# Eight instead of twelve shared units ahead of the experts, and the gather of their results in four parts

## What is computed

```
def _L1_cond_ref(x, router_logits, skill_gate, skill_up, skill_down, shared_gate, shared_up, shared_down):
    def _gemma_mlp(x, gate_w, up_w, down_w):
        g = jnp.einsum('bsh,hi->bsi', x, gate_w)
        u = jnp.einsum('bsh,hi->bsi', x, up_w)
        return jnp.einsum('bsi,ih->bsh', jax.nn.gelu(g, approximate=True) * u, down_w)
    rw = jax.nn.softmax(router_logits, axis=-1)
    w, sel = jax.lax.top_k(rw, 2)
    w = w / w.sum(axis=-1, keepdims=True)
    ...
    # out = sum over the two chosen experts of w * _gemma_mlp(x, ...)
    out = out + _gemma_mlp(x, shared_gate, shared_up, shared_down)
    return out
...
x = x + _L0_ffn_ref(_L0_cond_ref(x, ...), ...)
x = x + _L1_ffn_ref(_L1_cond_ref(x, ...), ...)     # act_qdq needs the largest |value| of its whole input
```

## Time and profile before

| | us |
|---|---|
| median of 3 runs | 492.7 (492.66 to 494.01) |
| the profiled execution, own time | 496.16 |
| its span, first to last instruction | 494.4 |
| PE busy | 388.2 (79%) |
| DVE busy | 337.5 (68%) |
| ACT busy | 268.0 (54%) |
| POOL busy | 253.1 (51%) |
| share of PE in the chain of work that ended last | 63% |
| mean granted clock of PE | 0.893 |

### The profile page before, as it was taken

The page is one execution under the profiler, slowest core; times in us unless marked ns, Lnnn a source line. Parts: engine busy times, 40 slices in busy tenths (PEclk is TensorE's granted clock), DMA queues, the critical chain, the costliest instruction groups (busy, mean ns, idle before and its releaser), DMA issues.

```text
span 494.4 us, 8506 instructions
## 1 busy us (share of the span) xinstructions
PE 388.2 (79%) x2550; PEld 340.5 (69%) x2550; DVE 337.5 (68%) x562; ACT 268.0 (54%) x402; POOL 253.1 (51%) x444
## 2 busy tenths in 40 slices
PE   2888948999999999999999999899487870000197
PEld 1655736779999999999999998676255640000197
DVE  2686546757789776776777766457555788979643
ACT  2565765655545445455454456454364688749360
POOL 2576841466677575665756201666134018976140
PEclk9997976999999999999999999899688995555599
DMA  8989770005776777767777515300000000000012
GB/s 268 356 267 315 247 297 1 1 0 204 264 254 230 278 237 256 262 233 272 245 241 273 205 34 196 156 1 1 0 0 0 1 0 0 0 1 0 0 65 106
DMA packets 31212, 71.26 MB, mean 144 GB/s; under 512 B 3904, under 2 KB 20032, under 8 KB 25920
## 3 DMA queue, kind: packets, MB, share of 16 engines
q1 hardware_dynamic: 28976, 66.33, 38.8%
q0 software_dynamic: 288, 4.19, 2.1%
q10 hardware_dynamic: 1904, 0.20, 0.3%
HBM read 55.12 MB, written 15.60 MB: 143 GB/s over the span
## 4 chain that ended last, share of the span: by engine, by line
PE 63%; DVE 18%; ACT 9%; POOL 4%; DMA 2%; issue 2%; ACTq 1%; POOLq 0%; DVEq 0%
PE ps L178 46%; PE ps L710 10%; DVE S L196 7%; DVE G L187 4%; PE ps L713 4%; PE ps L175 3%; DMA G<-yscr,sidx 2%; ACT G L184 1%; ACT ps L184 1%; POOL XCl L187 1%; ACT xnT L184 1%; ACT C_i L184 1%; POOL Hl L187 1%; ACT U L184 1%; DVE G L193 1%
## 5 line engine op out<-in xcount | busy, mean ns | idle before, releaser
L665 POOL CAST xg<-XT 128x64 fp32r x312 | 114.2, 413 | 60.2 <-PE ps L178 53.9
L184 ACT ACTIVATE Gb<-ps 128x512 f32<-128x512 f32 x110 | 65.8, 598 | 105.9 <-PE ps L178 105.2
L178 PE MATMUL ps<-xg,Wr 128*128 128x256 f32 x936 | 120.0, 284 | 0.0
L187 DVE TENSOR_TENSOR HbS<-Gb,ps 128x512 f32<-128x512 f32 x110 | 75.4, 686 | 62.4 <-PE ps L178 62.1
L178 PEld LDWEIGHTS ps<-xg,Wr 128*128 128x128 f32 x936 | 114.3, 190 | 0.1
L184 ACT ACTIVATE Hh<-HbS 128x512 fp32r<-128x512 f32 x110 | 68.9, 627 | 13.9 <-DVE HbS L187 13.9
L710 PE MATMUL ps<-WD,Hh 128*128 x312 | 74.3, 328 | 0.0
L713 PE MATMUL ps<-WD,Hl 128*128 x312 | 69.4, 223 | 0.0
L187 DVE TENSOR_TENSOR Hl<-HbS,Hh 128x512 fp32r<-128x512 f32 x90 | 65.1, 734 | 2.2
L713 PEld LDWEIGHTS ps<-WD,Hl 128*128 128x128 f32 x312 | 59.8, 192 | 0.0
L710 PEld LDWEIGHTS ps<-WD,Hh 128*128 128x128 f32 x312 | 59.0, 189 | 0.0
(11 more groups left out here) (181 smaller groups left out, 688.7 us busy)
## 6 DMA issues: line engine op xcount, KB each, us to landing
Wr<-wscr SPq DMA_DIRECT2D x39, 1024.0 KB, 5.1
wscr<-wst SPq DMA_DIRECT2D x16, 512.0 KB, 4.3
yscr<-Yb SPq DMA_DIRECT2D x39, 128.0 KB, 3.0
stg<-n_L_cond_skill_gate_dram SPq DMA_DIRECT2D x8, 256.0 KB, 5.7
stg<-in_L_cond_skill_up_dram SPq DMA_DIRECT2D x8, 256.0 KB, 3.8
stg<-n_L_cond_skill_down_dram SPq DMA_DIRECT2D x8, 256.0 KB, 4.4
out_dram<-X SPq DMA_DIRECT2D x7, 256.0 KB, 2.0
X<-in_x_dram SPq DMA_DIRECT2D x3, 512.0 KB, 6.5
```

What stands on the lines that cost most here:

```text
L178: return lambda e: e.matmul(o_, l, r, start=start, stop=stop, skip_group_check=True)
L184: return lambda e: e.activation(o_, i_, func, **kw)
L187: return lambda e: e.tensor_tensor(o_, a, b, op)
L665: k_xg[i] = pool.do(lambda e, s=s: e.tensor_copy(xg[:, i % XR, :, T * s:T * s + T], XT[:, :, :, bass.ds(regb[i][s], 1)].rearrange("p a t o ...
```

## The change

J0 goes from 3 to 2, so HK from 12 to 8: units 8 to 11 run behind the experts instead of ahead of them. EARLY goes from 6 to 4. The gather is cut into four parts of eight tokens (two groups j each), in the order of parts 2, 3, 0, 1; that makes eight indirect DMAs of 512 KB instead of two of 2 MB, each pair with its own semaphore, and needs eight index columns in `sidx` instead of two. Groups are weighed in every second step from 14 to 28, in the order 4, 5, 6, 7, 0, 1, 2, 3, and turned one step later. The weights' turns stay three steps behind HK.

```diff
-J0 = 3
-EARLY = J0 + 3
+J0 = 2
+EARLY = J0 + 2
...
                 if i == 4:
-                    tok["sidx"] = dve.do(cp(sidx[:, 0:2], S[:, 42:44]), d_)
+                    for p in range(4):
+                        tok["sidx"] = dve.do(ts(sidx[:, 2 * p:2 * p + 2], S[:, 42:44], 4.0, float(p), MUL, ADD), d_)
...
-        s_g = sem("s_g")
+        l_g = {}
         pool.wait(*y_tok, d_sidx, *moe_done)
-        l_g = None
-        for k, D in enumerate((G0, G1)):
-            l_g = pool.dma(lambda e, k=k, D=D: e.indirect_dma_start(
-                out=D[:, :, :].rearrange("p t c -> p (t c)"), out_offset=None, in_=yscr[:, :],
-                in_offset=bass.IndirectOffsetOnAxis(ap=sidx[:, k:k + 1], axis=0)), s_g, k + 1)
+        for p in (2, 3, 0, 1):
+            s_g = sem(f"s_g{p}")
+            for k, D in enumerate((G0, G1)):
+                l_g[p] = pool.dma(lambda e, k=k, D=D, p=p: e.indirect_dma_start(
+                    out=D[:, 8 * p:8 * p + 8, :].rearrange("p t c -> p (t c)"), out_offset=None,
+                    in_=yscr.rearrange("n (q c) -> (n q) c", q=4),
+                    in_offset=bass.IndirectOffsetOnAxis(ap=sidx[:, 2 * p + k:2 * p + k + 1], axis=0)), s_g, k + 1)
...
-            k_g[j] = pool.do(ts(flat(G0, j), flat(G0, j), S[:, 38:39], 0.0, MUL, ADD), l_g, d_w01)
+            k_g[j] = pool.do(ts(flat(G0, j), flat(G0, j), S[:, 38:39], 0.0, MUL, ADD), l_g[j // 2], d_w01)
...
-        weighs = {20: 0, 21: 1, 23: 2, 24: 6, 26: 3, 27: 7, 29: 4, 30: 5}
+        weighs = {14: 4, 16: 5, 18: 6, 20: 7, 22: 0, 24: 1, 26: 2, 28: 3}
+        turns = {n + 1: j for n, j in weighs.items()}
...
-            if n in (15, 16, 17):
-                turn_wf(n - 15)
+            if n in (11, 12, 13):
+                turn_wf(n - 11)
```

More of the change, by code:

```diff
@@ L802, in program @@
         a_wf, d_wf = {}, None
-        weighs = {20: 0, 21: 1, 23: 2, 24: 6, 26: 3, 27: 7, 29: 4, 30: 5}
-        turns = {21: 0, 22: 1, 24: 2, 25: 6, 27: 3, 28: 7, 30: 4, 31: 5}
-        largest = {22: 0, 23: 1, 25: 2, 28: 3, 30: 6, 31: 4, 32: 5}
+        weighs = {14: 4, 16: 5, 18: 6, 20: 7, 22: 0, 24: 1, 26: 2, 28: 3}
+        turns = {n + 1: j for n, j in weighs.items()}
+        largest = {22: 4, 24: 0, 26: 5, 27: 1, 28: 2, 30: 6, 31: 3}
         for n in range(HK, 34):
```

## The result

| | before | after |
|---|---|---|
| median of 4 runs, us | 493.36 (492.66 to 497.2) | 500.32 (498.65 to 501.31) |
| ratio after / before | | 1.0119, 95% interval 1.0072 to 1.0166 |
| profiled execution, own time | 496.16 | 500.99 |
| its span | 494.4 | 499.2 |
| start of up(7) | 97.78 | 96.32 |

The kernel became slower, by 7.0 us by the medians (interval 3.6 to 8.2) where 7.6 had been predicted. T is, as in the prediction, the start of the first step behind the experts. The marks add up in the profiled executions: -1.46 (the stage ahead of up(7)) - 4.35 + 12.88 - 2.33 = +4.74, the difference of the spans (4.8). The first of these is no effect of the change that can be told from chance: in the profiled executions of six kernels that are the same up to there, up(7) began between 96.32 and 98.79. Without it the change costs 6.2 us in the profiled execution.

A forecast was written before the change was run, and what follows sets the result against it. PE was taken to bound the kernel but for a few stalls. The terms -3.55 + 8.7 + 4.2 - 2.2 + 0.4 = +7.6 us, on the median of 492.7, gave 500.3 us; range for 8 in 10: 494.8 to 503.5.

The forecast's parts named there:

- What bounds the kernel: Whole kernel: PE bounds it but for a few stalls, and the change can win only those.
- Part 1: Start of the experts: units 8 to 11 leave the front, POOL's first fetch then bounds tile 0; gain 3.55 us.
- Parts 2 and 3: Behind the experts: four more units with a wait per turn cost 8.7 us; eight gather issues on POOL cost 4.2.
- Part 4: From up(31) to the last reduction: shorter, since the last turn is in step 29; gain 2.2 us.
- Part 5: Index cast to sidx on DVE: four operations instead of one; cost 0.4 us.
- its rival of 3.8 us: Index cast: with POOL busy without a gap, three more operations block, 3.8 us instead of 0.4; no chance given.
- Short issues: Gather issues: POOL is done by 308.83, so their delay costs nothing; 496.1 us; chance 25%.
- Parts together: Gather landing: all parts share the 12 us, the first complete only around 313; 502.6 us; chance 12%.
- Turns that don't wait: Behind the experts: splits, weighing and addition keep ahead of PE, a pair lasts 4.75 us; 489.7 us; chance 6%.

The follow-up runs named there:

- the kernel with the early fetch: Changed kernel with the splits of units 5 and 6 ahead of the experts on DVE instead of POOL; 496.72 us, ratio 1.0041.
- the kernel kept busy: Changed kernel with extra matmuls into an unread PSUM bank in PE's two pauses ahead of the first expert tile; 500.14 us.
- The two splits on DVE: Changed kernel with the splits of units 13 and 14 on DVE instead of POOL; 497.06 us, ratio 1.0057.
- J0 alone: Kernel before with only the four units moved (J0 = 2), gather in one piece and old tables; 494.23 us, ratio 0.9994.
- the version that beats both: Changed kernel with splits 5, 6 and those of steps 14, 15 and every weighing step on DVE, weighing one step later; 487.08 us, ratio 0.984.
- The kernel with parts and splits on DVE: Kernel before with J0 = 2, gather in four parts, old tables, splits of units 13 and 14 on DVE; 493.82 us, ratio 0.9995.
- parts alone: Kernel before with only the gather cut in four and eight index columns; 494.27 us, ratio 0.9992.
- the turns later: Changed kernel with each group turned two steps after its weighing instead of one; 496.45 us, ratio 1.0045.

## Why the prediction was right

- **What bounds the kernel: right.** Tile 2 to T is 179.27 us in both, and apart from the start, which varies, every difference lies at the places named. (The zeros of the earlier trace rows begin in slice 34, not 33, and slice 29 holds the end of the shared units too; nothing rests on it.)
- **Part 1, right in kind, mis-sized: -3.55 predicted, -4.35 measured.** The first fetch began where it was expected, 4.93 us behind the start of up(7), but took 1.89 us, where the term used the 2.44 of the earlier trace rows; fewer operations of DVE ran beside it, which may be why (I didn't test it). The two first tiles took 7.34 us, 7.5 predicted. The loss by the clock came in this execution, about 1 us. In two of the seven executions with these pauses it didn't, and there the gain was 5.3 us, beyond the 4.85 that the prediction gave as its far end, since the fetch is shorter. That the fetch bounds this place is shown by the kernel with the early fetch. That the pauses bring the clock's fall is likely from the counts, but the kernel kept busy alone doesn't show it.
- **Parts 2 and 3, right: T + 58.7 predicted, T + 58.65 measured.** The eight issues ended at T + 13.7 (T + 13.7 predicted), PE waited 2.11 us (2.3 predicted late), the addition lost its race and took 1.76 us (1.74), step 16 began at T + 18.06 (18.0), the next pair took 6.09 us (6.2), the others 5.39 with a wait of 0.50. The choice of 1.25 us an issue was right to 0.01 us. The two splits on DVE took 3.1 us of the cost away. What the prediction named wrongly is the owner of the 8.7 us. With J0 alone up(31) starts at T + 51.11, so the moved units have 5.3 of them, and the new tables 3.4, with a wait in each pair (the trace has seven waits for turns, one of them the late first one, where the kernel before has four). Part 4 belongs to the tables too: at J0 = 2 the end takes 8.19 us with the old ones.
- **Part 4, right:** 6.54 us, 6.6 predicted.
- **Part 5: 0.4 predicted.** The four operations took 1.49 us instead of 1.27, so 0.2 by the row: the first waited as before, and the other three fell into POOL's gap (1.42 us here), which is what the prediction said would keep its rival of 3.8 us away. The start of up(7) varies by more than 2 us from one execution to the next, and nothing of this size can be seen in it.

```profile
26.18 1.49 DVE L190 TENSOR_SCALAR sidx<-S 128x2 uint32<-128x2 f32 x4
```

- **The sum, and some luck:** 7.6 predicted, 6.2 in the profiled executions without the stage in front, 7.0 by the medians. Of the 1.4 between the first two, 0.8 stand in part 1, 0.1 in part 4, and 0.4 are part 5, which lies in the stage in front. That the median came out at 500.32 where 500.3 was forecast is luck in part. The forecast put its 7.6 on a median of 492.7 from three runs; beside the changed kernel it was 493.36, and 493.9 to 494.6 in the later runs, by which the change costs 5.8 to 6.5 us. The base was 0.7 us too low and the difference 0.6 us too high.
- **The rivals.** Short issues: excluded, 0.94 us each and 0.30 us of gap in front. Parts together: excluded, each of the eight landed 4.4 to 6.0 us after its issue, and the first weighing (306.53) waited for no data. Turns that don't wait: false here. It became true when the splits of the weighing steps went to DVE and the weighing one step later, in the version that beats both; the prediction said that nothing in the rows shortens this chain, and saw only the order as written.

## What to carry to other kernels

Starting a transfer isn't free for the engine that issues it (here 1.24 us of POOL for each gather): before a transfer is cut into more pieces, look at what stands behind the issues and when that is due, and move it to another engine. Two waits at one place don't add: take one away and the other may stand there, so price edits together and test the combinations. Where two engines' operations become ready within a tenth of a microsecond and slow each other, settle who comes first by the order of the program: here a lost race cost 1 us, more than the addition itself (0.75).

## What the hardware showed that was not expected

- **The size of a gather doesn't set its issue.** 128 rows of 4 KB and 128 rows of 16 KB both take 0.94 us on POOL, the first 1.22, with 0.30 us between; three issues in two kernels took 1.28 to 1.33 without a reason that the trace shows.
- **The clock falls only in some executions.** Behind the same two pauses (1.1 and 1.8 us) tiles 0 and 1 ran at full rate in two profiled executions and at half rate for a while in five; in the seven kernels without them (at most one pause of 0.8 us there) it never fell. The kernel with parts and splits on DVE is one of the two:

```profile
103.35 3.14 PE L178 MATMUL ps<-xg,Wr 128*128 128x256 f32 x24 [1.83 <-POOL xg L666]
```

  With half rate tile 2 came 16.0 us behind up(7), without it 15.04 and 15.05: about 1 us. Behind the experts the clock fell behind a pause of 1.98 us in the kernel before and behind 2.11 and 1.50 us in the changed one, but not behind 2.10 and 1.62 us with parts alone, nor behind a single one of 2.12 us with the turns later. Behind a pause of 3.60 us or more it fell each time, in three executions.
- **DVE's addition and POOL's split hold each other up.** Alone the addition takes 0.75 us and the split 1.29; where they meet one of them keeps its time, and the other takes longer: the addition 1.74 to 1.86, the split about 1.83. The Trainium skill, "SBUF — State Buffer", section "Who interferes with whom", says that a VectorE instruction with two inputs in SBUF contends with a GpSimd instruction that reads SBUF, and that the order of issue decides who blocks. The traces agree where the recorded starts are 0.06 us or more apart: POOL first, 14 times, and the addition was the slow one each time; DVE first, 49 times, and it kept its 0.75 us each time. With DVE recorded first by 0.04 or 0.05 us, four times, the addition was slow in three. That this race is also behind part of the spread from run to run (3.4 to 5.2 us within ten runs of one kernel) is likely, but wasn't shown.
